# Experts with more than 128 tokens: from second full tiles to two quads of 32-place lists on column tiles

## What is computed

```python
probs = jax.nn.softmax(logits.astype(jnp.float32), axis=-1)
rw, sel = jax.lax.top_k(probs, K)                       # K = 8 of E = 32
rw = rw / jnp.sum(rw, axis=-1, keepdims=True)
def body(acc, operand):
    e, wg, wu, wd = operand                             # 512x192, 512x192, 192x512
    w_e = jnp.sum(jnp.where(sel == e, rw, jnp.zeros_like(rw)), axis=-1)
    h = jax.nn.silu(x @ wg) * (x @ wu)
    return (acc + h @ wd * w_e[:, None], None)
...
h = h + _L0_ffn_ref(_layernorm(h, axis=-1), ...)
```

## Time and profile before

| | |
|---|---|
| median of 3 runs | 381.06 us (380.21 to 381.99) |
| the profiled execution: its own time | 377.78 us |
| its span, first to last instruction | 375.9 us |
| PE busy, share of the span | 84% |
| DVE, ACT, POOL busy | 42%, 36%, 42% |
| mean granted TensorE clock | 0.924 of full speed |

### The profile page before, as it was taken

How to read it: one execution, slowest core, us unless ns; L and a number is a source line. 1 busy time by engine, 2 the same in 40 slices (tenths; PEclk the granted TensorE clock), 3 DMA queues, 4 the chain that set the end, 5 groups by cost and what they waited for, 6 DMA issues and landing times.

```text
span 375.9 us, 4754 instructions
## 1 busy us (share of the span) xinstructions
PE 313.9 (84%) x1131; PEld 173.2 (46%) x1131; DVE 156.2 (42%) x465; ACT 137.0 (36%) x226; POOL 156.1 (42%) x144
## 2 busy tenths in 40 slices
PE   5799734558869469999999999999999999999910
PEld 1345211235536235555555555555555555555500
DVE  3348798174687833323322332332233233222102
ACT  3245738984873302222322322232232223223200
POOL 5304438643351122454355345435534543553230
PEclk9999976589989559999999999999999999999985
DMA  8599920097048331669999999999999999999667
GB/s 301 205 361 414 373 72 1 0 265 237 3 130 292 117 89 30 112 123 296 311 311 322 329 316 312 323 302 295 305 309 298 300 293 308 293 295 313 128 117 231
DMA packets 31310, 88.63 MB, mean 236 GB/s; under 512 B 4497, under 2 KB 4625, under 8 KB 30529
## 3 DMA queue, kind: packets, MB, share of 16 engines
q1 hardware_dynamic: 21936, 66.38, 51.7%
q0 software_dynamic: 8960, 21.63, 27.3%
q10 hardware_dynamic: 402, 0.48, 0.4%
HBM read 73.46 MB, written 15.02 MB: 235 GB/s over the span
## 4 chain that ended last, share of the span: by engine, by line
PE 66%; DVE 16%; ACT 5%; DMA 5%; issue 4%; POOL 2%; SPq 0%; DVEq 0%; POOLq 0%; ACTq 0%
PE ps L1025 30%; PE ps L1046 18%; PE ps L1035 5%; PE ps L1015 3%; DVE stats L1098 2%; PE ps L1054 2%; PE ps L901 2%; PE ps L851 2%; PE ps L927 2%; DMA sum<-w_t,add_idx 2%; ACT w_t L682 2%; DVE raw L1199 1%; POOL root_out L528 1%; DVE big L1193 1%; DVE amax L1246 1%
## 5 line engine op out<-in xcount | busy, mean ns | idle before, releaser
L599 POOL DMA_INDIRECT big<-token_rows,idx x40 | 39.6, 990 | 116.1 <-DVE idx L1338 98.0
L612 POOL DMA_INDIRECT sum<-w_t,add_idx x40 | 63.1, 1577 | 23.2 <-issue 13.0
L1388 DVE SCALAR_TENSOR_TENSOR w_t<-ps,big,w_t 128x192 f32<-128x192 f32 x40 | 16.7, 417 | 126.6 <-ACT w_t L812 126.6
L812 ACT ACTIVATE w_t<-ps 128x192 f32<-128x192 f32 x40 | 13.2, 331 | 109.9 <-PE ps L1025 109.9
L1025 PE MATMUL ps<-raw,w_t 128*128 128x384 f32 x144 | 51.1, 498 | 0.4 <-issue 0.4
L1025 PE MATMUL ps<-big,w_t 128*128 128x384 f32 x144 | 51.2, 499 | 0.0
L806 ACT ACTIVATE w_t<-ps 128x512 f32<-128x512 f32 x40 | 23.9, 597 | 47.6 <-PE ps L1046 47.6
L528 POOL TENSOR_TENSOR root_out<-root_in,minus_half 112x1 f32<-112x1 f32 x20 | 12.8, 640 | 59.1 <-DVE root_in L1111 59.0
L901 PE MATMUL ps<-w_t,q_t 128*112 128x512 bf16 (+1 forms) x96 | 26.1, 431 | 9.9 <-DVE h L1149 5.9
L1025 PEld LDWEIGHTS ps<-raw,w_t 128*128 128x128 f32 x144 | 25.9, 189 | 18.1 <-issue 3.8
L1025 PEld LDWEIGHTS ps<-big,w_t 128*128 128x128 f32 x144 | 25.9, 189 | 17.9 <-issue 3.6
(11 more groups left out here) (162 smaller groups left out, 397.7 us busy)
## 6 DMA issues: line engine op xcount, KB each, us to landing
big<-in_ffn_w_gate SPq DMA_DIRECT2D x18, 384.0 KB, 5.9
big<-in_ffn_w_up SPq DMA_DIRECT2D x18, 384.0 KB, 9.1
raw<-in_ffn_w_gate SPq DMA_DIRECT2D x18, 384.0 KB, 5.8
raw<-in_ffn_w_up SPq DMA_DIRECT2D x18, 384.0 KB, 7.1
raw<-in_ffn_w_down SPq DMA_DIRECT2D x18, 384.0 KB, 6.8
ring<-in_ffn_w_down SPq DMA_DIRECT2D x13, 384.0 KB, 7.2
big<-in_ffn_w_down SPq DMA_DIRECT2D x9, 384.0 KB, 7.5
big<-in_mlp_w_in SPq DMA_DIRECT2D x2, 1536.0 KB, 10.7
```

The source lines that it names most:

```text
L599: nc.gpsimd.indirect_dma_start(got[:, s, :], None, rows_dram[:, :], bass.IndirectOffsetOnAxis(ap=idx[:, s:s + 1], axis=0)).then_inc(ld_got ...
L612: nc.gpsimd.indirect_dma_start(acc_dram[n][:, :], bass.IndirectOffsetOnAxis(ap=add_idx[:, s:s + 1], axis=0), y[:, s, :], None, compute_op= ...
```

## The change

Each expert has one tile of 128 places, and these 32 tiles are written out without a loop and with fixed addresses. The tokens beyond 128 go to lists of 32 places; an expert with 129 to 160 tokens has one list. Four lists form a quad, whose 128 places are gathered, transposed and weighted like one tile. In `gate_up_lists` and `down_lists` each list is multiplied with its own expert's weights by matmuls that have 32 stationary columns and write 32 partitions of a PSUM bank, at partition 0, 32, 64 or 96 (four column tiles of the array). Quads are run in pairs in a loop; with eight lists there is one pair. The pair's `y` isn't scattered. DVE builds a matrix of zeros and ones, `where` (place by token), and PE multiplies `where` with `y` for each of the four groups of 112 tokens and sums both quads in PSUM (`spread_lists`). Meanwhile POOL loads the two sums of the scatters and adds them, and DVE adds PE's result to that.

The gate and up weights lie in one array, so that a tile has one transfer of 768 KB in place of two of 384 KB, with 6144 bytes for each partition in place of 3072 twice. There are eight weight slots in place of four and a half, and the load for tile t waits for tile t-8. The table of owners is worked out during tiles 3 to 7.

```diff
@@ SP: loads
-            def load_gate_up(slot, e, u):
-                sp.dma_start(slot[:, 0:WG // 2], we_gate_v[e, :, :]).then_inc(ld_gu[u], 16)
-                sp.dma_start(slot[:, WG // 2:WG], we_up_v[e, :, :]).then_inc(ld_gu[u], 16)
+            def load_gate_up(e, n):
+                sp.dma_start(slots[n][:, 0:WG], we_gate_up[e, :, :]).then_inc(ld_gu[n], 16)
...
+            for t in range(R, NE):
+                sp.wait_ge(gu_done, t - R + 1)
+                load_gate_up(t, t % R)
+                sp.wait_ge(y_done, t - R + 1)
+                load_down(t, t % R)
+            for k, n_pairs in pairs_of(sp, pairs_i, table_ready):
+                for n in range(R):
+                    e = sp.value_load(owner_row[0:1, bass.ds(8 * k + n, 1)], min_val=0, max_val=NE - 1)
+                    sp.wait_ge(gu_done, 8 * k + (NE - R + n + 1))
+                    load_gate_up(bass.ds(e, 1), n)
+                    sp.wait_ge(y_done, 8 * k + (NE - R + n + 1))
+                    load_down(bass.ds(e, 1), n)
...
@@ POOL
+            def gather(m):
+                s = m.four
+                pool.wait_ge(idx_ready, m.upto())
+                if isinstance(m, Quad):
+                    pool.wait_ge(hid_ready, m.upto(-2))
...
+            for t in range(NE):
+                if t + 3 < NE:
+                    gather(Tile(t + 3))
+                elif t + 3 < NE + 2:
+                    gather(Quad(0, t + 3 - NE))
+                if t:
+                    scatter(Tile(t - 1))
+            scatter(Tile(NE - 1))
+            for n in range(2):
+                pool.wait_ge(added[n], 16 * (NE // 2))
+                pool.dma_start(part[n][:, :, :], acc_dram[n][P:ROWS, :].rearrange("(g p) d -> p g d", g=NG)).then_inc(ld_part, 16)
+            pool.wait_ge(ld_part, 32)
+            for g in range(NG):
+                nc.gpsimd.tensor_tensor(part[0][:, g, :], part[0][:, g, :], part[1][:, g, :], ALU.add).then_inc(total_ready, 1)
...
@@ PE
+            def gate_up_lists(m):
+                pe.wait_ge(xt_ready, m.upto())
+                pe.wait_ge(hid_ready, m.upto(-2))
                 for c in range(4):
+                    for u in range(4):
+                        n, rows_ = 4 * m.i + u, slice(u * LIST, (u + 1) * LIST)
+                        if c == 0:
+                            pe.wait_ge(ld_gu[n], m.loaded())
+                        last = nc.tensor.matmul(bank(m.two)[rows_, 0:2 * IE].rearrange("p (n i) -> p n i", n=2),
+                                                x_t[:, m.two, c, rows_], gate_up_of(n)[:, :, c, :], start=c == 0, stop=c == 3)
...
+            def spread_lists(m):
+                pe.wait_ge(y_ready, m.upto())
+                pe.wait_ge(where_ready, 2 * m.k + (m.i + 1))
+                for g in range(NG):
+                    last = nc.tensor.matmul(bank(g)[0:G, :], where[:, m.i, g * G:(g + 1) * G], y_list[:, m.i, :],
+                                            start=m.i == 0, stop=m.i == 1)
...
-            pe.wait_ge(table_ready, 1)
...
+                if t == 4:
+                    pe.wait_ge(ht_ready, t)
+                    list_starts()
+                if t == 7:
+                    pe.wait_ge(ht_ready, t)
+                    list_tables()
...
+                if t == 7:
+                    pe.wait_ge(table_ready, 2)
+                transpose_h(Tile(t))
+            down(Tile(NE - 1))
+            for k, n_pairs in pairs_of(pe, pairs_i, table_ready):
+                a, b = Quad(k, 0), Quad(k, 1)
+                pe.wait_ge(fin_ready, 4 * k + 3)
+                transpose_x(a)
+                transpose_x(b)
+                gate_up_lists(a)
+                gate_up_lists(b)
+                transpose_h(a)
+                down_lists(a)
+                transpose_h(b)
+                place_lists(Quad(k + 1, 0))
+                spread_lists(a)
+                place_lists(Quad(k + 1, 1))
+                down_lists(b)
+                spread_lists(b)
...
@@ DVE, the pair
+                for m in two:
+                    dve.wait_ge(ld_got[m.four], m.gathered())
+                    for u in range(4):
+                        rows_ = slice(u * LIST, (u + 1) * LIST)
+                        e = dve.value_load(owner_row[0:1, bass.ds(m.first_list() + u, 1)], min_val=0, max_val=NE - 1)
+                        ins = nc.vector.tensor_copy(gate_w[rows_, m.i:m.i + 1], got[rows_, m.four, bass.ds(e + D, 1)])
+                    nc.vector.tensor_scalar(where[:, m.i, :], trow[:, :], idx_f[:, m.i:m.i + 1], None, ALU.is_equal
+                                            ).then_inc(where_ready, 1)
...
+                for m in two:
+                    weigh(m, gate_w[:, m.i:m.i + 1])
+                for m in two:
+                    turn_back(m)
+                for i in range(2):
+                    find(Quad(k + 1, i))
+                dve.wait_ge(total_ready, NG)
+                for g in range(NG):
+                    dve.wait_ge(spread_done, 4 * k + (g + 1))
+                    last = nc.vector.tensor_tensor(part[0][:, g, :], part[0][:, g, :], bank(g)[0:G, :], ALU.add)
+                    last.then_inc(fin_ready, 1)
```

More of the change, by code:

```diff
@@ L625, in _ @@
+            for i in range(2):
+                pool.wait_ge(ld_got[i], 16 * n_pairs + 16 * (NE // 4 + 1))
         @block.scalar
@@ L1003, in _ @@
             last.then_inc(rank_done, 1)
-            def place_row(st, d, b=7):
-                if st.beyond(d):
-                    return
-                t = st.tile(d)
-                wait(pe, idx_ready, st.upto(d - 1))
-                if isinstance(t, int):
-                    pick = ident16[0:NE, t:t + 1]
-                else:
-                    pick = owner[:, bass.ds(t, 1)]
-                nc.tensor.matmul(bank(b)[:, 0:TOK], pick.broadcast_to([NE, 128]), place[:, :], start=True, stop=True
-                                 ).then_inc(place_done, 1)
@@ new lines, in transpose_x, with down @@
+            def transpose_x(m):
+                pe.wait_ge(ld_got[m.four], m.gathered())
+                wait(pe, xt_ready, m.upto(-2))
+                for c in range(4):
+                    last = nc.tensor.transpose(bank(2 + m.two)[:, c * P:(c + 1) * P], got[:, m.four, c:D:4], ident[:, :])
+                last.then_inc(xt_done, 1)
+            def down(m):
+                wd = down_of(m.slot)
+                pe.wait_ge(ht_ready, m.upto())
+                pe.wait_ge(ld_dn[m.slot], m.loaded())
+                wait(pe, y_ready, m.upto(-2))
@@ L1045, in down, with down_lists @@
                 for c in range(2):
[L1046 to L1047 removed]
+                    last = nc.tensor.matmul(bank(4 + m.two), h_t[:, m.two, c, :], wd[:, c, :], start=c == 0, stop=c == 1)
                 last.then_inc(y_done, 1)
[L1050 to L1052 removed]
+            def down_lists(m):
+                pe.wait_ge(ht_ready, m.upto())
+                pe.wait_ge(y_ready, m.upto(-2))
@@ L1071, in _ @@
-            nc.tensor.matmul(bank(1)[0:1, NT:2 * NT], iota_e16[:, :], owner[:, :], start=True, stop=True
-                             ).then_inc(tables_done, 1)
-            pe.wait_ge(idx_ready, 3)
-            pe.wait_ge(table_ready, 1)
-            for st in steps_from(pe, more_i, more_ready):
-                place_row(st, 3)
-                gate_up(st)
-                transpose_x(st, 1)
-                down(st, -1)
-                transpose_h(st)
-            down(Step(st.k, U - 1), 0)
+            transpose_x(Tile(0))
```

498 lines of the change are left out of this document (254 added, 244 removed).

## The result

The changed kernel takes 359.6 us (median of 4 runs, 358.37 to 360.77) beside 380.63 for the kernel before (4 runs): a ratio of 0.9463, with a 95% interval of 0.9398 to 0.9529. Its profiled execution took 358.37 us and has a span of 356.4. The forecast was 358, and the span was to be 353.1. The number was nearly met, but not by the way that was given for it, as the trace shows.

The account below looks back on a forecast made before the run. PE was taken to bound the kernel, at 5.48 us a tile, with a tail behind. S 308.5 plus a 44.6 us tail gave span 353.1, 22.8 less; from the 381.06 median, 358 us, range 350 to 376.

Parts of the forecast that it names:

- S: Start of tile 31's gate_up, from which the new tail is counted: 308.07 before, forecast 308.5.
- The likeliest case: Lists' products on PE overlap only between neighbouring lists: 5.7 us per quad's gate_up, 358 us in all; chance 0.50.
- rival 1: Lists' products on PE: all four column tiles run abreast, POOL's sums and DVE's adds end the kernel, 353.1 us; chance 0.17.
- The rule weighed: Lists' products: skill page's column-tile speedup implied near 2.7 us per quad's gate_up; its weight-load rule implied bare loads.
- The wait for the table: PE held before the loop's first place row; 0.8 us gained by dropping table_ready.
- I leave the clock high: PE's clock stays high through its idle 3.3 us before the second quad's transposition.
- Slack 4.7: POOL's sums ready at 33.5, 4.7 us before DVE needs them at 38.2, so the scatter tail hides behind the quads.
- From the last add to the end: End of the kernel, after DVE's last add: the store as before, 3.1 us.
- Serial: Lists' products on PE: column tiles don't overlap at all, 374.4 us; chance 0.18.
- bare loads: Lists' products: serial, with 96 uncovered weight loads adding 8.6 us, 383.0 us, slower; chance 0.05.
- The loop does not wait for gathers: Denies the tile-loop rival: gathers landing later than 8.2 us delay each tile, 364 us; chance 0.07.
- A ninth list: Quads: rounding gives one expert another token, hence a second pair, about 388 us; chance 0.03, shared with something else.

Follow-up runs that it names:

- e9: e8 with the lists' gate, up and down matmuls written list by list, as in e4: 351.55 us, tail 38.2.
- e4: The changed kernel with the lists' gate, up and down matmuls written list by list: 359.48 us, tail 46.5.
- e1: The changed kernel without POOL's gathers for a next pair of quads and the wait for them: 352.93 us, tail 40.2.
- e2: The changed kernel with the first two quads' gathers waiting for the hid of tiles 28 and 29, not 30 and 31: 356.64 us, tail 42.5.
- e3: The changed kernel with both edits, of e1 and e2: 345.87 us, tail 34.7; run again 347.12 us, tail 34.9.
- e5: The changed kernel without quads and all that serves them, so tokens beyond an expert's first 128 get nothing from it: 344.85 us, tail 33.5.
- e6: e3 with the two sums loaded by SP in four pieces each and added on DVE, not POOL: 346.84 us, tail 34.4.
- e8: e7 with DVE's adds of the sums put between its two find calls: 346.0 us, tail 33.5.
- e7: e6 with the second quad's down_lists ahead of the first quad's spread_lists on PE: 347.67 us, tail 34.5.

## Why the prediction was right, and where it was wrong

**The time** (358, measured 359.6) and the sign were right. The tiles were worth what the distance between them says, and the old tail of 67.8 us became one of 47.3: 20.5 less, of which the later S gives 1.0 back, 19.5 in the span (forecast 22.8). That the number was met is luck, as the points below show.

**The likeliest case was wrong, and rival 1 (full overlap) right.** The step that failed is "only the second of one list and the first of the next can overlap. That makes 17 steps of 0.336, 5.7 us", with its ground, "instructions on PE start in their order in every row I read". Those rows had no instructions side by side in different column tiles, so they couldn't show it. There PE lets an instruction go past earlier ones that wait for another column tile. A quad's products take 8 steps of 0.32, 2.7 us; `down_lists` 1.92 and not 3.9. e9 shows the passing itself, and that its reach is short: with eight instructions to a list two lists run abreast, with four to a list (`down_lists` in e4) all four. Read as a short queue for each column tile, of about four instructions, filled in program order, both follow; that reading is argued from the two cases, not tested with a third.

**The rule weighed.** The Trainium skill, page "TensorE: Matmul & The Clock Gate", section Measured speedup vs the span model, has 2.38 times for three column tiles. Here four give the full factor of four in their starts, and the price that the prediction took from that section, near 2.7 us for a quad, is the measured one. The total of the rival with that price, 353.1, was still further from 359.6 than the forecast, since it too lacks the end behind the last add. The Trainium skill's rule in the section The mechanism of the same page, that a weight load overlaps only where row groups differ, would have bared the lists' loads. The trace disagrees: in the window 326.4 to 329.1 PE's matmuls are busy for all 2.70 us, with the weight loads (0.84) under them, though all lists share the rows. That section of the Trainium skill also says that matmuls are never reordered, in the same spirit as my premise; the pairs of e9 contradict it for different column tiles.

**Point by point,** in us after S, forecast first:
- S itself: 308.5 and 309.07. The wait for the table is gone, but its 0.8 can't be read from two profiles: tile 4 came 0.37 earlier, and in the profiles of the changed kernel and e1 to e9, with the same stages ahead, the first tile starts anywhere from 135.4 to 139.5. The tables in tiles 4 and 7 cost 1.8 and not 1.2, of which tile 31 without its place row gives 0.4 back.
- The second quad's gather issued at 4.1 and 4.4, landed at 10.6 and 12.2: it took 7.8, more than the 7.4 of the earlier trace rows.
- PE's wait: 3.3 and 4.6. "I leave the clock high" was wrong. It fell to 0.70 in the wait and was 0.63 in the first quad, which cost PE 1.45 us (4.24 against the 2.79 of e2), though not the kernel, whose end hung on POOL. The earlier trace rows had shown an idle stretch at 0.99, but here the fall came within the wait. The next window of the same idle time of before would have warned, for there the clock is at the lower level:
```profile
363.00:368.00 5.00, 0.00 (x0) 0.00 (x0) 0.00 (x0) 0.00 (x0) 0.00 (x0) 0.50 0.90 238
```
- DVE's weights of the second quad: 17.3 and 17.1. The gather landed 1.6 later, but DVE's reads of the owners' numbers came 0.83 apart, where 1.05 was taken.
- End of both `gate_up_lists`: 22.5 and 20.0. End of PE: 40.7 and 34.7.
- POOL: scatter 31 issued at 14.6 and 15.8, landed at 20.6 and 20.6. The sum's load came at 26.7 and 29.1: a load of 896 KB on POOL's queue takes 8 to 9 us to land, with the other sum's in flight for part of it, where the forecast took 2 to issue and the 3.84 of the earlier trace rows. Its adds were 1.24 each, not 1.7. Sums ready at 33.5 and 34.0.
- "Slack 4.7" for POOL was therefore none: PE was early and POOL on time, so POOL became the last before the adds. Rival 1 has this, and its last add at 36.3 is measured at 36.6.
- From the last add to the end: 3.1 and 10.7. This is the term that no case had. In the forecast it was the store's time alone, and POOL was followed only up to its sums. What it issues behind them was left out: two gathers for a pair that never comes, the wait for them, and its closing instruction of 5.8 us. e1 prices it at 7.1 us. The trace of before held the hint: GpSimd's closing instruction ends at 370.10, 3.3 us after the last scatter landed, with no row in the views.

So an error of 4.9 us too much ahead of the last add, and one of 7.6 too little behind it, left the sum 3.3 short with S counted in. The right number here does not speak for the working.

**The other rivals.** Serial and bare loads are ruled out by the steps of 0.32. The loop does not wait for gathers: PE is busy for 54.00 of 54.00 us. A ninth list would show a second pair of quads, and there is none.

**Where the rest of the gain went.** The removed tiles leave a tail that could be 33.5 us and was 47.3. Of those 13.8, 12.6 lie in two places: the unneeded gathers with the closing instruction behind them (7.1 alone) and the late gather with the scatters behind it (4.8 alone). The other 1.2 are the difference between e3 and e5; e6 to e8, with the sums off POOL and other orders on PE and DVE, took as much away, from 34.7 to 33.5.

## What to carry to other kernels

Follow every engine to its last instruction, not only to its last useful one. Here work issued for a next round that doesn't come sat on the end of the kernel. Compare each engine's last row with the span's end, and ask what fills the rest.

When small matmuls go to different column tiles, write them so that neighbours in program order lie in different tiles. Here that gave four abreast; list by list gave two where a list had eight instructions, and still four where it had four.

When an engine is moved forward, look at what stands ahead of the consumer in its own queue: in e7 a `find` for data that nobody needs held the adds that PE had been sped up for.

## What was not expected of the hardware

- Four column tiles of float32 matmuls run fully abreast: 32 instructions in 2.7 us, where the 8 of a full-width `gate_up` take 2.7 too. Across column tiles PE does not keep program order (e9).
- GpSimd's closing instruction takes 5.8 us in the changed kernel, e2 and e4, where it comes behind a wait; behind GpSimd's adds it ends 5.6 us after the last in e1 and 5.5 in e5. On the other engines but TensorE it takes 0.8 us at most in the records above. Before, the other engines' work hid it.
- The same load of a sum takes 8 to 9 us to land as one DMA of 896 KB from POOL's queue (by the DMA issues below; 8.3 is POOL's wait for it in e5). In four pieces from SP in e8 the chain shows 6.80 for the last, and the earlier trace rows 3.84 before. How much of it is the queue, how much the size and how much the other sum's load, in flight beside it, was not separated. The rows of the changed kernel (count, KB, us to landing):
```profile
h<-sum POOLq DMA_DIRECT2D x1, 896.0 KB, 9.0
big<-sum POOLq DMA_DIRECT2D x1, 896.0 KB, 8.1
...
out<-h ACTq DMA_DIRECT2D x2, 224.0 KB, 4.2
```
- With PE idle for 4.6 us behind the tiles the clock fell to its lower level; where the wait was 0.75, as in e8, the window of both quads shows 1.00:
```profile
317.90:324.50 6.60, 6.19 (x64) 2.13 (x64) 2.37 (x10) 0.81 (x2) 1.55 (x1) 1.00 1.01 269
```
